# Head keys in quarters and values stored twice: a fused attention, expert and scan kernel with its PSUM banks dealt out anew

## The reference

```python
# 1: attention over the 16 images at each position, 8 heads of 16 channels
zn = layernorm(x) * ln_w + ln_b
q, k, v = zn @ Wq, zn @ Wk, zn @ Wv          # ln_b @ Wv is a constant row of v
g = sigmoid(zn @ Wg + bg)
att = softmax(einsum('iabhc,jabhc->ijabh', q, k) / sqrt(16), axis=1)
x = x + (einsum('ijabh,jabhc->iabhc', att, v) * g) @ Wo + bo
# 2: top 2 of 8 experts for each position
x = x + mixture(layernorm(x), router_w, expert_w)
# 3: expansion to 128 channels; half of them through an exponential moving average along the
#    first spatial axis, then a sigmoid gate on the other half
x = x + (primary * sigmoid(ema(gating))) @ W_con.T + b_con
# 4: for each image, 32 experts pick their 8 best positions, a small MLP, scattered back
x = x + picked_mlp(layernorm(x))
```

## Time and profile before

| | us |
|---|---|
| median of three runs | 3134.15 |
| the profiled execution, its own time | 3123.18 |
| its span | 3121.5 |
| PE busy | 2647.5 (85%) |
| DVE busy | 2551.6 (82%) |
| POOL busy | 2161.0 (69%) |
| ACT busy | 2005.1 (64%) |

### The profile page before, as it was taken

How to read it: one execution, slowest core, us unless ns; L and a number is a source line. 1 busy time by engine, 2 the same in 40 slices (tenths; PEclk the granted TensorE clock), 3 DMA queues, 4 the chain that set the end, 5 groups by cost and what they waited for, 6 DMA issues and landing times. The chain is left out here.

```text
span 3121.5 us, 108500 instructions
## 1 busy us (share of the span) xinstructions
PE 2647.5 (85%) x37071; PEld 1969.9 (63%) x37071; DVE 2551.6 (82%) x9002; ACT 2005.1 (64%) x3590; POOL 2161.0 (69%) x2963
## 2 busy tenths in 40 slices
PE   2898898888888888898898898888988988896697
PEld 2666666666666656666666666666666666664586
DVE  2788889888888898888888888888889888885604
ACT  2666767766676676776776766677667676762600
POOL 2677777877777777777787877778777777863000
PEclk9788988887888888888887987889889788885858
DMA  0011101111011010110101111011010010101828
GB/s 17 9 20 18 19 17 19 19 18 19 17 19 18 18 19 17 19 19 18 19 17 18 19 18 19 17 19 19 18 19 18 17 19 18 19 15 19 269 96 337
DMA packets 263153, 106.67 MB, mean 34 GB/s; under 512 B 250257, under 2 KB 254900, under 8 KB 258997
## 3 DMA queue, kind: packets, MB, share of 16 engines
q1 hardware_dynamic: 260933, 93.16, 12.9%
q10 hardware_dynamic: 2160, 12.68, 1.0%
HBM read 55.31 MB, written 50.33 MB: 34 GB/s over the span
## 5 line engine op out<-in xcount | busy, mean ns | idle before, releaser
L472 ACT ACTIVATE kT<-s_bank,b_k,block_of 128x512 f32<-128x512 f32 x1024 | 748.8, 771 | 3.6 <-PE s_bank L609 0.3
L640 PE MATMUL s_bank<-kT,qT 128*32 128x128 f32 x8192 | 396.1, 372 | 187.3 <-issue 187.3
L640 PEld LDWEIGHTS s_bank<-kT,qT 128*32 128x32 f32 x8192 | 349.5, 152 | 226.8 <-issue 224.7
L489 ACT ACTIVATE qT<-shared,b_qkg 128x256 f32<-128x256 f32 x256 | 107.5, 471 | 412.0 <-PE shared L609 412.0
L811 DVE TENSOR_REDUCE mixed<-yg 128x256 f32<-128x2048 f32 x128 | 288.5, 2254 | 0.2
L687 PEld LDWEIGHTS o_bank<-w_o,ogT 128*128 128x128 f32 x2048 | 247.9, 193 | 23.7 <-DVE ogT L839 14.8
L414 POOL TENSOR_TENSOR probs<-weights,own_den 128x1024 f32<-128x1024 f32 x128 | 252.7, 1975 | 1.8 <-DVE own_den L857 1.8
L687 PE MATMUL o_bank<-w_o,ogT 128*128 128x64 f32 x2048 | 246.9, 274 | 4.3 <-DVE ogT L839 3.9
L387 POOL TENSOR_TENSOR split_ffn<-norm_ffn,split_ffn 128x256 fp32r<-128x256 f32 x128 | 93.6, 731 | 215.1 <-ACT split_ffn L464 215.1
L658 PEld LDWEIGHTS o_bank<-probsT,v_sb 32*32 32x32 f32 x16384 | 170.2, 107 | 63.7 <-issue 58.1
L658 PE MATMUL o_bank<-probsT,v_sb 32*32 32x64 f32 x16384 | 196.5, 234 | 1.5 <-DVE yg L932 1.5
(11 more groups left out here) (204 smaller groups left out, 7648.6 us busy)
## 6 DMA issues: line engine op xcount, KB each, us to landing
x_in<-in_x SPq DMA_DIRECT2D x1024, 16.0 KB, 1.7
x_scratch<-x SPq DMA_DIRECT2D x1024, 16.0 KB, 1.4
normalized_x_scratch<-norm_pick SPq DMA_DIRECT2D x1024, 16.0 KB, 1.5
xa<-normalized_x_scratch SPq DMA_DIRECT2D x16, 1024.0 KB, 8.1
xb<-x_scratch ACTq DMA_DIRECT2D x8, 1024.0 KB, 10.3
out_x<-xa SPq DMA_DIRECT2D x16, 512.0 KB, 5.3
out_x<-xb SPq DMA_DIRECT2D x16, 512.0 KB, 6.9
xa<-x_scratch SPq DMA_DIRECT2D x4, 1024.0 KB, 6.5
```

Source lines behind the costliest of these rows:

```text
L472: ins = s.activation(kT[:, h, :], bk("k")[:], ACT.Identity, bias=b_k[:, h:h + 1], scale=block_of[:, h:h + 1])
L640: ins = t_.matmul(s_bank[g * 32:(g + 1) * 32, 0, t * P:(t + 1) * P], qT[z][:, c, tok:tok + 32], kT[:, :, tok + c * N:tok + (c + 1) * N], s ...
```

## The change

The scores are computed in 64-row halves of the array: heads 0 to 3 from channels 0 to 63 and heads 4 to 7 from channels 64 to 127, so four masked copies of the keys do (each keeps 16 channels in either half), and a matmul moves 64 columns instead of 128. v is stored with each head of a pair beside 16 zeros, once for the first head and once for the second; two value matmuls of 32 columns then add up in PSUM to an output without a wrong half. v's constant row goes in by a matmul of three bf16 rows. `own_den` moves from DVE to POOL. The scores use the values' banks, which frees two, and the other steps share four banks by a fixed table `BANK`. Several steps stand elsewhere in the order of their engine.

```diff
-TURNS = ["att_t", "q", "ffn_t", "v", "scan_out", "gate", "pick", "conv_t", "y0", "expand", "y3"]
-BORROWED = {"y2": ("o", 0), "att_out": ("o", 1), "pick_t": ("o", 2), "route": ("o", 3),
-            "y1": ("s", 0), "k": ("s", 1)}
+TURNS = ["att_t", "q", "ffn_t", "scan_out", "gate", "k", "pick_t", "v", "route", "pick", "conv_t", "y0", "expand",
+         "att_out", "y1", "y2", "y3"]
+BANK = {"att_t": 0, "q": 1, "ffn_t": 2, "v": 3, "scan_out": 0, "gate": 1, "k": 2, "pick_t": 3, "route": 0, "pick": 1,
+        "conv_t": 3, "y0": 1, "expand": 3, "att_out": 0, "y1": 1, "y2": 2, "y3": 3}
...
@@ POOL @@
-                        pool.wait_ge(drained["v"], at(i, q, 1))
-                        g.tensor_tensor(v_sb[z][:], v_sb[z][:], bv_rows[:].unsqueeze(1).broadcast_to([P, QT, HC]),
-                                        ALU.add).then_inc(s_v, 1)
...
                         pool.wait_ge(s_rden, at(i, q, 2))
+                        g.tensor_tensor(own_den[:], ssum[:].unsqueeze(2).broadcast_to([P, 32, 2]),
+                                        odd_even[:].unsqueeze(1).broadcast_to([P, 32, 2]), ALU.mult).then_inc(s_own, 1)
@@ ACT @@
-                        s.copy(v_sb[z1][:].rearrange("p t c -> p (t c)"), bk("v")[:]).then_inc(drained["v"], 1)
...
+                        for h in range(2):
+                            ins = s.copy(v_sb[z1][:, :, h, :, h, :],
+                                         bk("v")[:].rearrange("p (t k h c) -> p t k h c", k=4, h=2, c=C)[:, :, :, h, :])
+                        ins.then_inc(drained["v"], 1)
...
-                        masked_keys(range(4, 6))
+                        masked_keys(range(2, 4)).then_inc(drained["k"], 1)
...
-                        masked_keys(range(6, 7))
...
-                        masked_keys(range(7, H)).then_inc(drained["k"], 1)
@@ PE @@
-                                    ins = t_.matmul(s_bank[g * 32:(g + 1) * 32, 0, t * P:(t + 1) * P],
-                                                    qT[z][:, c, tok:tok + 32], kT[:, :, tok + c * N:tok + (c + 1) * N],
-                                                    start=(c == 0), stop=(c == 1), tile_position=(0, g * 32))
+                                    for u in range(2):
+                                        tok, rows = t * P + g * 32, slice(u * D, (u + 1) * D)
+                                        ins = t_.matmul(o_bank[g * 32:(g + 1) * 32, u, t * D:(t + 1) * D],
+                                                        qT[z][rows, c, tok:tok + 32],
+                                                        kT[rows, :, tok + c * N:tok + (c + 1) * N],
+                                                        start=(c == 0), stop=(c == 1), tile_position=(u * D, g * 32))
...
+                        wait_apart(pe, (s_probsT, at(i, q, 3)), (drained["v"], at(i, q, 3)), (s_og, at(i, q, 4)),
+                                   (s_sub, at(i, q, 2) if runs(i, q, 2) else HALVES))
+                        pT = probsT[:].rearrange("p (u t m) i -> p u t m i", u=2, t=QT)
+                        for t in range(QT):
+                            for h in range(2):
+                                for k in range(4):
+                                    for g in range(4):
+                                        ins = t_.matmul(o_bank[k * 32:(k + 1) * 32, g, t * 32:(t + 1) * 32],
+                                                        v_sb[z][g * 32:(g + 1) * 32, t, h, k].rearrange("p h c -> p (h c)"),
+                                                        pT[g * 32:(g + 1) * 32, k // 2, t, 2 * (k % 2) + h, :],
+                                                        start=(h == 0), stop=(h == 1), tile_position=(g * 32, k * 32))
...
+                        t_.matmul(bk("v")[:], ones3[:], bv3[:], start=True, stop=False)
...
+                            ins = t_.matmul(bk("att_out")[:, t * D:(t + 1) * D], ogT[:, tile(t)], w_o_half[:])
@@ DVE @@
-                        for h in range(2):
-                            o = o_bank[:, :, 0:QT * 64].rearrange("p g (t h i) -> p g t h i", h=2, i=32)[:, :, :, h, :]
-                            ins = v.tensor_tensor(by_group(ogT[:, h, :]), o, by_group(gT[z][:]), ALU.mult)
+                        o = o_bank[:, :, 0:P].rearrange("p g (t i) -> p g t i", i=32)
+                        v.tensor_tensor(by_group(ogT[:]), o, by_group(gT[z][:]), ALU.mult).then_inc(s_og, 1)
```

198 lines of the change are left out of this document (90 added, 108 removed).

## The result

The changed kernel took 4786.75 us (median of 4 runs, 4779.61 to 4795.67), the kernel before beside it 3137.73 (3130.02 to 3146.6): 1.5255 times as long, interval 1.52 to 1.5311. The forecast was 3050. The profiled execution spans 4794.0 us against 3121.5, at a mean clock of 0.606 against 0.839.

A forecast was written before the change was run, and what follows sets the result against it. An ACT-PE ring set the 21.57 us slot, with DVE the next limit. DVE's path of 17.88 busy, 1.1 gaps, 1.15 and 0.5 waits and 0.3 clock gave 20.9 us a slot, 3050 us; range with rivals 2950 to 3130.

The forecast's parts named there:

- The ring of key copies and scores: One `kT` buffer and one key-projection bank tie ACT's 11.36 us and PE's 9.92 into the 21.3 us slot; the change opens it.
- DVE's busy time: On DVE, per slot: 19.05 us falls to 17.88, by 0.64 for one `ogT` and 0.53 for `own_den` leaving.
- Maxima and subtraction from two banks: On DVE, the same elements read from two banks instead of one: taken as 0 extra, bounds 0 and 0.2 us.
- `y1`'s wait behind DVE: `y0` and `y1` share a bank, so DVE stands 1.15 us at the full clock or 1.85 at the half.
- `sel`'s: DVE's wait at `sel` for ACT's `lge`: 0 to 1.2 us, taken as 0.5.
- half-clock case: The three matmuls of `y1` take 1.76 us at the half clock; with the hand-overs DVE stands 1.85 us.
- A new wait: PE may begin `y1` only after DVE has multiplied `y0` in the same bank; DVE stands 1.15 or 1.85 us.
- A second one, smaller: In the router's chain, ACT's `lge` is ready at S + 7.6, `sel` could start at S + 6.9; wait taken as 0.5 us.
- the sum: DVE's path: 17.88 busy, 1.1 gaps, 1.15 and 0.5 waits, 0.3 half clock: 20.9 us a slot, 3050 us in all.
- Nothing gained: Rival: another ring of the same length takes over, through the later add and POOL's normalization; 3125 to 3145 us; chance 0.11.
- four signs that it gave for being wrong: Values above 4 us; DVE's largest wait at `lg` or maxima; mean clock below 0.8; PE waiting for `split_ffn` in most slots.
- Slower, by the values: Rival: values between subtraction and `lg` take longer: 3400 us at 25 ns each, 3330 at a mostly low clock; chance 0.12.

The follow-up runs named there:

- e5: The kernel before with four key copies instead of eight and half-width scores, nothing else changed: 3048.98 us, 0.972 of the kernel before.
- e3: The changed kernel with POOL's `x_bo` moved to the end of its slot and ACT's `gT` behind v's copies, `lT` ahead of `split_conv`: 4409.81 us, 1.4102.
- e4: The changed kernel with the two moves of e3 and half of the values left out, as in e2: 3723.96 us, 1.1909 of the kernel before.
- e2: The changed kernel without the second value matmul of each pair, so half of the values is left out: 4266.01 us, 1.3642 of the kernel before.
- e8: The kernel before with its value matmuls issued twice, 403 matmul instructions a slot: 3218.41 us, 1.0281 of the kernel before.
- e15: The kernel before with its value matmuls issued two and a quarter times, 435 matmul instructions a slot: 3597.09 us, 1.1479 of the kernel before.
- e14: The kernel before with its value matmuls issued two and a half times, 467 matmul instructions a slot: 3972.72 us, 1.2678 of the kernel before.
- e13: The kernel before with both halves of the change (those of e5 and e12), in the old order and banks: 3767.05 us, 1.2001 of the kernel before.
- e6: e4 plus twelve unused 3-row bf16 matmuls a slot, eight ahead of the key projection and four ahead of `y1`: 3812.28 us, 1.2178 of the kernel before.
- e9: e4 with ACT's copy `tT` moved ahead of `split_att`: 3609.51 us, 1.1531 of the kernel before.
- e10: e4 plus four unused float32 matmuls of 256 columns and all 128 rows ahead of the key projection: 3584.64 us, 1.1425 of the kernel before.
- e12: The kernel before with values stored twice, compact output, one `ogT`, four output projections and v's bias by matmul, old order and banks: 3256.35 us, 1.0384.
- e7: e9 with the output projection right behind the router's pick on PE and the attention's add with its statistics ahead of `yg` on DVE: 3466.84 us, 1.1049.

## Why the prediction was wrong

**What was right.** The ring of key copies and scores opened (e5). DVE's busy time was 17.5 us a slot, forecast 17.88. Maxima and subtraction from two banks cost nothing extra (681 ns for the maxima, 687 before). The value matmuls are busy 2.94 us a slot (167.5 / 57), forecast 2.9. The Trainium skill, "TensorE: Matmul & The Clock Gate", Back-to-back issue gap, gives at least 25 ns from start to start, by which 256 would take 6.4 us (an estimate from that figure); the trace again disagrees. POOL had `norm_conv` ready at 1528.66, 4.6 us after the end of the subtraction, forecast 4.3. `y1`'s wait behind DVE was there, `sel`'s too (0.8, forecast 0.5). The length of `y1`'s wait was the one in the text's half-clock case and more: 3.3 us a slot (356.7 / 108), because the output projection's 1.80 us stand on PE between the draining of `y0` and `y1`, and `y1` runs at half speed. The step *A new wait* counted from DVE's draining of the bank to the end of `y1` and left out what stands on PE between.

**The step that failed: what stands in front of `split_conv` and `lT` on ACT.** *A second one, smaller* lets ACT run `split_conv`, `lT` and v's copies as soon as POOL has `norm_conv`, at S + 4.3, and PE give the router's logits at S + 5.2, S being the end of DVE's subtraction. But `gT` stands in front of them on ACT and waits for `ogT` (`o_gated`) of the slot in progress, that is for the end of the values. In the slot shown S is 1524.02: the values start at S + 2.2 and end at S + 8.8, stops included, `gT` starts at S + 9.7, `lT` at S + 11.2, v's projection, whose bank `lT` must drain, at S + 11.9, and DVE gets the logits at S + 16.0. POOL's `x_bo`, which waits for the add of the slot in progress in the same way, isn't in the sum at all; of POOL it says "not in the path". Both waits stood in the old order too and cost next to nothing, 20.2 us in 102 slots for `gT` and none for `x_bo`, since `ogT` and the add came early. With values, `ogT` and the add moved towards the slot's end, the same two lines became 7.7 and 10.1 us of waiting. e3, which takes the two out of their places, gives 377 us of the 1650, and e4 against e2 542; the rest of what the order costs is not in these two waits alone.

The rival *Nothing gained* named the right engine and edge, POOL's normalization for `ffn_t` behind the add, and put the ring at "about 20 us, with errors of 1 us". The slot is 35.2. The prediction doesn't write that walk out, so which of the measured links it lacked can't be said; it has neither `x_bo` nor `gT`.

Three of the four signs that it gave for being wrong came: DVE's largest wait was at `lg`, the mean clock was 0.606, and PE waited for `split_ffn` in 57 of 57 slots. The fourth, values above 4 us, came only by the stops: 2.94 us of work in 6.6 us.

**The missing term: instructions.** Under *PE* the sum priced 185 more matmul instructions a slot by their duration, and the fetching had no row: the trace of before shows none in the loop (none from 500 to 2700 us, 40 in the run). e8, e15 and e14 show that the time of the same code grows by 5.2 us a slot (660 us / 128) between 403 and 467 instructions a slot beyond what the work costs, and e13 that the change pays nearly as much, 0.19 or 4.7 us a slot, without its new order.

**The mis-sized term: the clock.** The sum added 0.3 us with the clock at half speed for 28% of the time. It is there for (1 - 0.59) / 0.5 = 82%. The rival *Slower, by the values* had this as a condition ("a clock that stays low in more than half of the slots") at 3330 us, with its chance taken mostly from the values; it held three short stops harmless since none would be as long as 2.44 us. In the slot shown three are longer: 2.79 us before `ffn_t`, 2.75 inside the values, 3.04 before v's projection. That the stops keep the clock low isn't shown, for e6 fills e4's 2.6 us pause ahead of the key projection with work, e9 removes it, and the clock is 0.65 and 0.67. What the low clock costs is bounded from one side only, by e10's 139 us.

How the 1650 us divide, in the order in which the experiments take them: keys alone -88; values alone, by e12's ratio, +120; the fetching that the two bring together, e13, some +600; the new order and banks the remaining 1020 (4787 - 3767), of which the two waits are 377 and the steps of e9 and e7 may be 257 more, measured with half of the values missing. The rest of it, nearly 400 us, was not taken apart. No run has the new banks without the new order, or the whole of the values in the new order without fetching, and the clock's part isn't separated from either.
